# Layers 0 and 1: the q and k projections of a token block are issued piece by piece between the attention heads of the block before

## The reference, cut to what matters

```python
h = shift_token(x)                       # upper half of the features from the token before
q, k, v = split(h @ wqkv)                # 1024 -> 3 x 512, 8 heads of 64
q = l2norm(q) * qs ; k = l2norm(k) * ksc
q, k = rotary_xpos(q, k)
# windows of 512 tokens, each looks at itself and the window before, at most 512 back
sim = einsum('bhwid,bhwjd->bhwij', q * 8, k)
attn = softmax(where(mask, -max, sim))
x = x + (attn @ v) @ wo
h = layernorm(shift_token(x)); a, g = split(h @ w1 + b1); x = x + (a * gelu(g)) @ w2 + b2
```

## Time and profile before

| | us |
|---|---|
| timed runs | 12534.5 and 12739.7, median 12637.1 |
| profiled execution, its own time | 12550.3 |
| its span, slowest core (core 2) | 12548.7 |
| spans of the eight cores | 12407.5 to 12548.7 |
| windowed attention, layer 0 (from 2782 in the span) | 2667 |
| windowed attention, layer 1 (from 7635) | 2401 |

### The profile page before, as it was taken

One profiled execution on the slowest core, in us unless ns is written; L12 is line 12 of the kernel. 1 busy time (PEld: TensorE's weight loads), 2 busy tenths in 40 slices (PEclk: granted clock), 3 DMA queues, 4 the chain that ended last, 5 costly groups with the idle time before them and its releaser, 6 DMA issues.

```text
span 12548.7 us, 88354 instructions; the slowest of 8 cores (12407.5 to 12548.7 us)
## 1 busy us (share of the span) xinstructions
PE 7596.9 (61%) x31326; PEld 3019.7 (24%) x31830; DVE 4059.8 (32%) x6588; ACT 1649.8 (13%) x2895; POOL 92.9 (1%) x139
## 2 busy tenths in 40 slices
PE   0588445445665666656778874566655657688731
PEld 0233112112222222223223222222222223222211
DVE  0111233335444544431221113444444431111224
ACT  0001111111111112110001000111211210000100
POOL 1000000000000000000000000000000000000000
PEclk9999777765555555567898776555555556788965
DMA  9302100010000000001222222000000000122221
GB/s 119 42 3 23 23 3 10 7 23 2 1 1 1 2 1 1 0 13 24 59 62 67 52 59 51 2 1 1 1 1 1 1 11 22 51 67 55 56 66 50
DMA packets 610701, 326.38 MB, mean 26 GB/s; under 512 B 489492, under 2 KB 541316, under 8 KB 608736
## 3 DMA queue, kind: packets, MB, share of 16 engines
q0 software_dynamic: 65344, 79.31, 5.1%
q1 hardware_dynamic: 310496, 137.55, 4.3%
q10 hardware_dynamic: 234432, 103.83, 3.3%
HBM read 374.48 MB, written 59.77 MB: 35 GB/s over the span
## 4 chain that ended last, share of the span: by engine, by line
PE 46%; DVE 28%; DMA 8%; issue 7%; ACT 6%; another core or an unknown queue 3%; DVEq 1%; ACTq 0%; POOL 0%; SPq 0%; POOLq 0%
PE M0b L1541 6%; PE M1b L1541 5%; DMA w2b<-w2bf 4%; DVE mcol L1110 3%; DMA w1g<-w1bf 3%; PE kps L488 2%; PE L1b L978 2%; PE L0b L978 2%; DVE L0b L1272 2%; PE vps L499 2%; PE M0b L1598 2%; DVE L1b L1272 2%; PE M1b L1598 2%; PE p2b L749 2%
## 5 line engine op out<-in xcount | busy, mean ns | idle before, releaser
L1598 PE MATMUL M0b<-hbuf,w2b 128*128 128x512 bf16 (+1 forms) x1728 | 436.4, 406 | 159.1 <-DMA w2b<-w2bf 105.3
L1541 PE MATMUL M0b<-xt,w1a 128*128 128x512 bf16 (+1 forms) x1709 | 463.6, 421 | 101.8 <-DVE xt L1500 70.5
L978 PE MATMUL L0b<-wqkv_l,X_g 128*128 128x512 bf16 x938 | 295.6, 478 | 329.6 <-DVE ubuf L1037 143.9
L978 PE MATMUL L1b<-wqkv_l,X_g 128*128 128x512 bf16 x937 | 295.1, 479 | 330.0 <-DVE ubuf L1037 149.4
L1574 DVE SCALAR_TENSOR_TENSOR hbuf<-M0b,gout 128x512 bf16<-128x512 f32 x220 | 143.4, 652 | 1045.8 <-ACT gout L1566 1034.3
L1541 PE MATMUL M0b<-xt,w1g 128*128 128x512 bf16 (+1 forms) x1726 | 437.0, 401 | 44.6 <-DMA w1g<-w1bf 40.2
L1541 PE MATMUL M1b<-xt,w1a 128*128 128x512 bf16 x1365 | 409.7, 451 | 87.4 <-DVE xt L1500 57.8
L1598 PE MATMUL M1b<-hbuf,w2b 128*128 128x512 bf16 x1380 | 356.1, 407 | 123.9 <-DMA w2b<-w2bf 79.6
L488 PE MATMUL kps<-WkSb,X_g 128*128 128x512 bf16 x616 | 172.7, 429 | 425.1 <-DMA WvSb<-Wv 418.7
L1574 DVE SCALAR_TENSOR_TENSOR hbuf<-M1b,gout 128x512 bf16<-128x512 f32 x176 | 121.8, 692 | 896.4 <-ACT gout L1566 886.9
L1541 PE MATMUL M1b<-xt,w1g 128*128 128x512 bf16 x1381 | 368.9, 413 | 14.7 <-DMA w1g<-w1bf 10.8
(11 more groups left out here) (391 smaller groups left out, 12421.8 us busy)
## 6 DMA issues: line engine op xcount, KB each, us to landing
w1a<-w1bf SPq DMA_DIRECT2D x198, 256.0 KB, 3.2
w1g<-w1bf ACTq DMA_DIRECT2D x198, 256.0 KB, 3.4
w2b<-w2bf SPq DMA_DIRECT2D x198, 256.0 KB, 2.6
w2b<-w2bf ACTq DMA_DIRECT2D x198, 256.0 KB, 2.6
w1bf<-w POOLq DMA_DIRECT2D x8, 2816.0 KB, 203.6
outT<-fin_o SPq DMA_DIRECT2D x32, 512.0 KB, 3.5
w2bf<-w POOLq DMA_DIRECT2D x8, 1408.0 KB, 274.1
X_g<-x_extT POOLq DMA_DIRECT2D x4, 2624.0 KB, 41.5
```

The lines of the kernel that those rows point to most:

```text
L978: mm = s.add("tensor", lambda t, c=c, part=part, bank=bank, tc=tc, off=off, st=(c == 0): t.matmul(bank[:, :], sb["X"][:, c, tc + off:tc + ...
L1541: mm = s.add("tensor", lambda t, banks=banks, wt=wt, half=half, fin=fin, nn=nn, st=(fin == 0): t.matmul(banks[half][:, 0:nn], wt[:, fin, : ...
L1598: mm = s.add("tensor", lambda t, c=c, j=j, sl=sl, half=half, nn=nn, st=(j == 0), sp=(j == 21): t.matmul(P[c][:, 0:nn], w2b[sl][:, 128 * c: ...
```

## The change

For blocks 2 to 9, stage 1 is taken apart. `piece_v` computes v alone, in stage 1, all four groups into P[6], each waiting for the cast of the one before. The q and k of block w + 1 are computed during the attention of turn w: behind head h = 2j stands `piece_q` of group j, behind head 2j + 1 `piece_k` of group j, and ahead of each following q piece, and behind head 7, `piece_T`, the transposes of the finished pair. Both pieces use P[2], the bank of the replicated row of sums, so their matmuls wait for the head's last product. The squares go to a new SBUF tile `xqk` in bf16 rather than to P[5]. Both halves of the transposes go through P[4]. Blocks 0 and 1 are still done as a stage, with v first and then q and k in turn through P[2]; there `piece_T` stands ahead of the next group's q. The output product uses P[6] and P[7]. CL is 1 in both layers. The tables of rotations of block w + 1 are loaded ahead of the heads of turn w.

```diff
-            pcol0, n_proj, qcol0, CL = 128, 10, 640, 2
+            pcol0, n_proj, qcol0, CL = 128, 10, 640, 1
...
+            xqk = self.sbuf(f"xqk{l}", (128, 512), BF16, es)
...
+            def piece_v(pw):
+                slot = pw % 3
+                for j in range(4):
...
+                        mm = s.add("tensor", lambda t, c=c, tc=tc, off=off, st=(c == 0): t.matmul(
+                            P[6][:, :], sb["X"][:, c, tc + off:tc + off + 128],
+                            wqkv[:, c, 1024:1536],
+                            start=st, stop=(c == NCH - 1)), deps)
+                    t_vevac[slot] = s.add("vector", lambda v, slot=slot, j=j: v.tensor_copy(
...
+            def piece_q(pw, j):
...
+                    if c == 0:
+                        deps = deps0 + [t_uq, t_tt1, t_sqred[0]]
+                    mm = s.add("tensor", lambda t, c=c, tc=tc, off=off, st=(c == 0): t.matmul(
+                        P[2][:, :], sb["X"][:, c, tc + off:tc + off + 128],
+                        wqkv[:, c, 0:512],
...
+                t_qsqr = s.add("scalar", lambda sc: sc.activation(
+                    xqk[:, :], P[2][:, :], AF.Square), [mm, t_qrd])
+                rd = s.add("vector", lambda v: v.tensor_reduce(
+                    bnf[:, 0:8], xqk[:, :].rearrange("p (h d) -> p h d", d=64),
+                    AX.X, ALU.add), [t_qsqr])
+                t_qrd = rd
+                sq = s.add("scalar", lambda sc: sc.activation(
+                    bnf[:, 8:16], bnf[:, 0:8], AF.Sqrt), [rd])
...
             for w in range(n_iter):
-                blk = pcol0 + 512 * w
                 slot = w % 3
...
+                if w < n_proj and w <= CL:
+                    piece_tab(w)
+                    piece_v(w)
+                    pend = None
                     for j in range(4):
...
+                        if pend is not None:
+                            piece_T(w, pend[0], pend[1], pend[2])
+                        tqt = piece_q(w, j)
+                        tkt = piece_k(w, j)
+                        pend = (j, tqt, tkt)
+                    piece_T(w, pend[0], pend[1], pend[2])
+                elif w < n_proj:
+                    piece_v(w)
...
+                    pw = w + 1
+                    il = (CL < pw < n_proj)
+                    if il:
+                        piece_tab(pw)
...
+                        if il:
+                            ph = h
+                            jj = ph // 2
+                            if ph % 2 == 0:
+                                if pend_il is not None:
+                                    piece_T(pw, pend_il[0], pend_il[1], pend_il[2])
+                                    pend_il = None
+                                self._tq_il = piece_q(pw, jj)
+                            else:
+                                tkt = piece_k(pw, jj)
+                                pend_il = (jj, self._tq_il, tkt)
+                    if il:
+                        piece_T(pw, pend_il[0], pend_il[1], pend_il[2])
...
-                            pbk = c % 2
+                            wbank = P[6] if c % 2 == 0 else P[7]
```

More of the change, by code:

```diff
@@ L912, in build_layer, with piece_tab @@
             t_stmm = None
+            def piece_tab(pw):
+                nonlocal t_tab
+                t_tab = s.dma("gpsimd", tabs[:, :, :, :],
+                              inp["tab"][pcol0 + 512 * pw:pcol0 + 512 * pw + 512, :, :]
+                              .rearrange("(j p) a d -> p j a d", p=128),
+                              dtab, deps=[t_tabuse])
+            def piece_v(pw):
+                slot = pw % 3
+                for j in range(4):
+                    tc = pcol0 + 512 * pw + 128 * j
+                    mm = None
+                    for c in range(NCH):
+                        off = -1 if c >= 4 else 0
+                        deps = []
+                        if c == 0:
+                            deps = [t_vevac.get(slot), t_tt1, t_mcopy, t_wo, t_w,
+                                    self.t_p2 if l == 0 else
+                                    getattr(self, "t_halofix", None),
+                                    getattr(self, "_dbg_tok", None)]
+                            if pw == 0 and j == 0:
+                                deps = deps + gate
+                        mm = s.add("tensor", lambda t, c=c, tc=tc, off=off, st=(c == 0): t.matmul(
[3 more added lines that the diff above has]
+                    t_vevac[slot] = s.add("vector", lambda v, slot=slot, j=j: v.tensor_copy(
+                        bass.AP(vt[slot], 520 * j, [[4 * 520, 128], [65, 8], [1, 64]]),
+                        P[6][:, :].rearrange("p (h m) -> p h m", m=64)),
+                        [mm, t_init, t_mcopy, t_pv, getattr(self, "_dbg_tok", None)])
@@ new lines, in piece_k @@
+            def piece_k(pw, j):
+                nonlocal t_projmm, t_ksq_last, t_qrd, t_uk, t_tabuse
+                tc = pcol0 + 512 * pw + 128 * j
+                mm = None
+                for c in range(NCH):
+                    off = -1 if c >= 4 else 0
+                    deps = []
+                    if c == 0:
+                        deps = [t_uk, t_uq, t_tt1]
+                    mm = s.add("tensor", lambda t, c=c, tc=tc, off=off, st=(c == 0): t.matmul(
+                        P[2][:, :], sb["X"][:, c, tc + off:tc + off + 128],
+                        wqkv[:, c, 512:1024],
+                        start=st, stop=(c == NCH - 1)), deps)
+                t_projmm = mm
+                tks = s.add("scalar", lambda sc: sc.activation(
+                    xqk[:, :], P[2][:, :], AF.Square), [mm, t_qrd])
+                t_ksq_last = tks
+                rd = s.add("vector", lambda v: v.tensor_reduce(
+                    bnf[:, 16:24], xqk[:, :].rearrange("p (h d) -> p h d", d=64),
+                    AX.X, ALU.add), [tks])
+                t_qrd = rd
+                sq = s.add("scalar", lambda sc: sc.activation(
+                    bnf[:, 16:24], bnf[:, 16:24], AF.Sqrt), [rd])
+                mx = s.add("vector", lambda v: v.tensor_scalar(
+                    bnf[:, 16:24], bnf[:, 16:24], 1e-12, None, ALU.max), [sq])
+                rc = s.add("vector", lambda v: v.reciprocal(
+                    bnf[:, 16:24], bnf[:, 16:24]), [mx])
+                t1 = s.add("vector", lambda v: v.tensor_tensor(
+                    ubuf[:, :], P[2][:, :],
+                    bass.AP(bnf, 16, [[24, 128], [1, 8], [0, 64]]),
+                    ALU.mult), [rc])
+                t_uk = t1
+                t2 = s.add("vector", lambda v: v.tensor_mul(
+                    qhat[:, :], ubuf[:, :], ks_rep[:, :]), [t1])
+                ta = s.add("vector", lambda v, j=j: v.tensor_tensor(
+                    ubuf[:, :], qhat[:, :],
+                    bass.AP(tabs, 256 * j + 2 * DF, [[4 * 4 * DF, 128], [0, 8], [1, DF]]),
+                    ALU.mult), [t2])
+                tb = s.add("vector", lambda v, j=j: v.tensor_tensor(
+                    krot[:, :].rearrange("p (h t x) -> p h t x", h=8, t=2),
+                    bass.AP(qhat, 32, [[512, 128], [64, 8], [-32, 2], [1, 32]]),
+                    bass.AP(tabs, 256 * j + 3 * DF, [[4 * 4 * DF, 128], [0, 8], [32, 2], [1, 32]]),
+                    ALU.mult), [ta, self.t_ttk])
+                tk = s.add("vector", lambda v: v.tensor_add(
+                    krot[:, :], krot[:, :], ubuf[:, :]), [tb])
+                t_tabuse = tk
+                return tk
@@ L1254, in build_layer @@
                                         sb["zrow"][0:1, 0:512], start=True, stop=False),
-                                        [t_oacc])
+                                        [t_oacc, t_wo])
                             if pend is not None:
```

241 lines of the change are left out of this document (84 added, 157 removed).

## The result

| | us |
|---|---|
| before, median of 42 timed runs | 12568.1 |
| after, median of 43 timed runs | 12613.6 |
| after / before | 1.0054, 95% interval 1.0027 to 1.0081 |
| profiled execution of after, its own time | 12531.3 |
| its span, slowest core (core 4) | 12529.8 |

What follows compares the result with a forecast made beforehand. No engine is full; windowed attention is a chain of hand-overs between DVE, PE and ACT. Layer 0 +74, layer 1 +64 and +1, blocks 0 and 1 +65: 204 us on 12550.3 gives 12754, range 12710 to 12830.

Steps and rivals of the forecast that it cites:

- head with a piece: Attention heads with a q or k piece behind them: 22.65 us from head to head against 14.75.
- heads of layer 1's first turn: Heads without a left half or reciprocal: 14.6 us with a piece against 9.0; at three heads transposes add 2.8.
- last product to output product behind head 7: After the eighth head, k's transposes precede the output product: it starts at 12.0 us, 11.8 more than before.
- v stage: Stage before the row maxima, now v alone: 17.0 us at 1.2 GHz replaces 74.9, saving 57.9 per iteration.
- stage of blocks 0 and 1: Projection stages of blocks 0 and 1, v first, q and k sharing one bank: +65 us in both layers together.
- What no row shows: Prediction's section on unmeasured assumptions: cost of bf16 squares in SBUF, and 1.2 GHz for pieces, output product and v.
- The 7.9 us of a head: Between heads in interleaved turns: the piece and table switches add 7.9 us per head, 22.65 against 14.75.
- the bf16 squares change nothing: Square to SBUF and its reduce keep 1.46 us from Square start to load start; otherwise -39 to +77 over 112 places.
- Rival 1: Exp load right after Sqrt: ACT empties first, 1.28 us more at 112 places, +143, 12897 us; chance 0.13.
- Rival 2: Pair's transposes slip behind the last product: 2.8 us at 3 heads x 15 iterations, +126, 12880 us; chance 0.05.
- Rival 3: Clock rises in attention and holds over value products: 2.3 us back at 105 heads, 242, 12512 us; chance 0.15.
- Rival 4: As rival 3, with pieces at 2.4 GHz too: 1.7 us more at 128 pieces, 218, 12294 us; chance 0.09.

Runs made afterwards that it cites:

- the run with 0.41: A small DVE memset between the fourth and fifth matmul of each v group, a pause of 0.41 us, against the changed kernel: 12736.8 us, one run.
- With 0.87 in v: A 65x512 DVE memset between the fourth and fifth matmul of each v group, a pause of 0.87 us, against the changed kernel: 12763.3 us, one run.

## Why the prediction was wrong

By its own steps, in us:

| step | forecast | measured | difference |
|---|---|---|---|
| head with a piece, 105 of them | 22.65 | 22.57 | -8 |
| heads of layer 1's first turn, 7 | 14.6, three with 2.8 more | 13.7 to 14.6, three of 17.1 to 17.3 | -2 |
| last product to output product behind head 7 | 12.0 | 11.6 to 12.0 | -2 |
| v stage, 16 turns | 17.0 | 11.5 to 13.6, sum 192 | -80 |
| stage of blocks 0 and 1 | +65 | +44 | -21 |
| output product, 10 groups of four at the higher clock | 1.9 each | 1.0 to 1.4 | -8 |
| last turns, without pieces | 0 | +4 | +4 |

The terms are those of core 4; the smaller CL and the tables ahead show no cost. They leave 87 of the 204, and the stages show 89 to 93. In layer 0 they leave +52, measured +52 to +53; in layer 1 +35, measured +36 to +40. On the other cores the v stages of the 16 turns sum to 193 to 201. Two errors of the account are small: banks 6 and 7 aren't free in a turn without pieces, where the output product waits for the save of P[7] (L1315) and starts 0.8 us later than in before (a part of the +4; the rest was not traced), and the sum had no term for a rise of the clock in the output product.

**The step that failed** is in "What no row shows": a run of the projection's matmuls rises from 0.50 to 1.00 only after about ten of them; "A piece has eight, the output product and v four and eight between waits, so I take 1.2 GHz for all of it." For the output product it held in 140 of 150 groups of four, which took 1.9 with pauses of 0.94. For v it did not. As a rule only its first run of eight was at 0.50, and the three others took 1.89 instead of 3.57 each, 5.0 us less; no turn reached 17.0, the longest on any core being 15.3. I had read the ten matmuls off one unbroken run and taken its length for a condition, though that row shows only when that run rose, not that a pause starts the count anew. After's own v stages show that a pause of 0.95 need not, and the run with 0.41 that a rise comes with runs of four too. With 0.87 in v the clock never rose there, and then the v stage is the 17.0 of the forecast and the pauses, and the start stages are its 65 and the pauses. So that v's clock is worth the 80 us, and the 21 of the start stages, is shown by this. Why the clock rises in v after all is not: no run here gives a rule that fits all the turns.

A higher clock was priced in the wrong place: in rivals 3 and 4 for the heads, at 242 us and more, and not for v, where 32 matmuls with three short pauses were the nearest thing to the earlier trace rows. An end of its own for it, -5.3 x 16 = -85 us, would have carried the forecast's own range down to 12625, which is +0.6% on that execution and close to what was measured.

**What held.** The 7.9 us of a head: its account (piece behind the last product, Square, reduce, load, Sqrt, load, Exp) stands row by row in the timeline, and both parts are shown by taking them away: 3.8 us a head without the loads, 3.8 in four of seven heads with a bank of its own. So ACT's chain was on the path as said. That the bf16 squares change nothing: the reduce is 0.69 from SBUF too. The counts: loads went from one pair per turn to eight.

**The rivals.** Rival 1, a switch costs more when ACT has just worked: Sqrt ends at 3931.01, the load starts at 3931.02 and takes 1.28, and Exp starts 1.30 behind its start. It fell. The Trainium skill (ScalarE: Activation LUTs, "What ACT_TABLE_LOAD costs") gives 1283 ns for the load, and 259 loads have that mean; the drain of about 1380 ns that it puts beside it does not show in this place. Rival 2, transposes uncovered: in the head shown above the piece starts 0.14 behind the last product, but no transposes stand ahead of it there; behind head 2 of the same turn k's transposes end 1.3 us before the last product does:

```profile
3967.34 1.08 PE L1064 MATMUL L0b<-identF_g,krot 128*128 128x128 f32 x4 [0.82 <-ACT qf L1054]
...
3969.04 0.68 DVE L1310 TENSOR_TENSOR osb<-tsum,L0b 64x512 bf16<-64x512 f32 x1
```

Heads 2, 4 and 6 are 22.5 apart like the others, and on core 0 all 120 pieces behind a last product start 0.15 us after it. It fell. Rival 3 was half right: the clock did rise behind the piece, but it was down again, after the wait for the loads, before the value products; where the loads were taken away it held in about half of the heads, and gave 2.1 of the 2.3 us that the rival had worked out there and 1.3 on average. Rival 4 fell: on core 0 90 of the 128 pieces take 3.57, the time of 1.2 GHz, and none less than 3.0.

## What to carry to other kernels

Work put into the gaps of a chain is not hidden if it shares with the chain something that is waited for: here a bank and a function table made it a serial step. With both the kernel is 0.5% slower than before; without the shared bank it is 1.8% faster, without the table 3.1%, and without either 5.6%. A sum over matmuls with short waits between them has two prices, one at each clock level, and the second belongs into the range as an end of its own. Run the parts of a change apart: here a stage rebuilt so that it could be taken apart cost 1.5%, and taking it apart gave back 1%, which the total of +0.54% doesn't tell.

## What the runs showed of the hardware

- Short pauses did not keep TensorE's clock down reliably, and no one pause or length of run told when it rose. Runs of eight 512-column matmuls with pauses of 0.95 us rose to 2.4 GHz in all 16 interleaved turns, on each of the eight cores. Runs of four with a pause of 0.41 in the middle rose after 8 to 16 matmuls in nine of 16 turns on core 4, and never in six. Runs of four in v with pauses of 0.87 and 0.95 in turn rose in none, on no core. But the output product, also in fours with pauses of 0.94, rose for 10 of 150 groups on after's core 4 and fell back after two to four of them; in the kernel before it rose for none on any core:

```profile
9622.64 1.02 PE L1347 MATMUL L1b<-osb,wo_l 128*128 128x512 bf16 x4 [0.94 <-DVE X_g L1351]
...
9631.26 1.86 PE L1347 MATMUL L1b<-osb,wo_l 128*128 128x512 bf16 x4 [0.94 <-DVE X_g L1351]
```

  In the first stage of layer 0 the runs of eight did not rise on core 4 until the q piece followed v without a pause:

```profile
2840.62 3.57 PE L937 MATMUL L0b<-wqkv_l,X_g 128*128 128x512 bf16 x8 [20.55 <-DVE vt L941]
...
2849.65 3.57 PE L937 MATMUL L0b<-wqkv_l,X_g 128*128 128x512 bf16 x8 [0.95 <-DVE vt L941]
2853.02 1.98 PE L957 MATMUL L0b<-wqkv_l,X_g 128*128 128x512 bf16 x8
```

  Why the same pattern rises in one place and not in the other stays open. PE had waited 20.55 us ahead of this one, and 0.94 ahead of the v stage of a later turn; but on core 0 the same stage rose in its fourth run of eight, and in layer 1 on core 4, behind a wait of 21.0 us, in the third.
- A table load costs more than its 1.28 us where PE waits for it: 3.8 us a head on average for two loads of 2.57 together. With them the clock was 0.50 over the value products in all 105 heads and these took 6.5 us; without them they took 4.4 in the 50 heads where the clock was 1.00, and 5.2 on average.
- Nothing beside the load itself showed at a switch of tables: Sqrt ends at 3931.01, the load starts 0.01 later, and Exp starts 1.30 behind its start.
